# Three PSUM banks of the v blocks and one SyncE transfer are moved in a cross-attention and feed-forward kernel

## The reference

```python
# x [8, 256, 256], ctx [8, 77, 256], 16 heads of 64
x = x + xattn(layernorm(x), ctx)     # LN with gamma, beta inside; then
                                     # q = xn @ w_q; k, v = split(ctx @ w_kv)
                                     # softmax(q k^T / 8) v; @ w_out + b_out; * tanh(gate)
x = x + ffn(layernorm(x))            # (silu(x wg^T) * (x wu^T)) wd^T, 256 -> 768 -> 256,
                                     # int32 weights times 1/127
```

## Time and profile before

| what | value |
|---|---|
| median of 3 runs | 317.37 us (316.65 to 319.08) |
| profiled execution | 316.46 us, span of its instructions 314.6 us |
| TensorE matmul busy | 298.3 us, 95% |
| VectorE, ScalarE, GpSimd busy | 235.3, 172.2, 167.0 us |
| granted clock of TensorE | 0.999 |
| DMA | 23.29 MB, mean 74 GB/s |

### The profile page before, as it was taken

The page is one execution under the profiler, slowest core; times in us unless marked ns, Lnnn a source line. Parts: engine busy times, 40 slices in busy tenths (PEclk is TensorE's granted clock), DMA queues, the critical chain, the costliest instruction groups (busy, mean ns, idle before and its releaser), DMA issues.

```text
span 314.6 us, 6453 instructions
## 1 busy us (share of the span) xinstructions
PE 298.3 (95%) x2399; PEld 275.8 (88%) x2399; DVE 235.3 (75%) x622; ACT 172.2 (55%) x338; POOL 167.0 (53%) x170
## 2 busy tenths in 40 slices
PE   7799999897987999999999999999999999989896
PEld 7798977686885999889988989898999889978896
DVE  1298887596785887878887797778787878784873
ACT  4356874658325852773486249535942772465142
POOL 2390863347853871668096629644771668045042
PEclk9999999999999999999999999999999999999999
DMA  6993153512414021102201120202020101100001
GB/s 201 387 361 84 35 205 138 174 52 102 138 55 118 2 73 35 33 3 74 68 0 32 44 69 0 76 0 69 1 77 33 35 0 43 56 13 0 2 0 70
DMA packets 16314, 23.29 MB, mean 74 GB/s; under 512 B 1634, under 2 KB 13898, under 8 KB 16282
## 3 DMA queue, kind: packets, MB, share of 16 engines
q1 hardware_dynamic: 16282, 22.85, 22.3%
HBM read 15.87 MB, written 4.62 MB: 65 GB/s over the span
## 4 chain that ended last, share of the span: by engine, by line
PE 80%; POOL 10%; issue 3%; DVE 2%; ACT 2%; DMA 2%; SPq 0%; POOLq 0%; ACTq 0%; DVEq 0%
PE ps L825 11%; PE ps L771 8%; PE ps L757 7%; PE ps L731 5%; PE ps L739 5%; PE ps L735 5%; PE ps L658 4%; PE ps L886 4%; PE ps L890 4%; PE ps L887 4%; PE ps L844 3%; PE ps L873 3%; PE ps L870 3%; POOL probs L1127 3%; POOL t_lo L1134 3%
## 5 line engine op out<-in xcount | busy, mean ns | idle before, releaser
L1127 POOL TENSOR_TENSOR probs<-probs,total 128x616 f32<-128x616 f32 x32 | 39.1, 1221 | 75.7 <-DVE total L1260 75.7
L978 ACT COPY pt<-ps 77x512 f32<-77x512 f32 x64 | 34.2, 584 | 49.2 <-PE ps L757 49.2
L1134 POOL TENSOR_TENSOR t_lo<-t_all,t_hi 128x1232 fp32r<-128x1232 f32 x16 | 45.6, 2849 | 4.7 <-ACT t_hi L1003 4.7
L1143 POOL TENSOR_TENSOR h_lo<-hid,h_hi 128x256 fp32r<-128x256 f32 x42 | 31.0, 737 | 28.4 <-ACT h_hi L1053 28.4
L757 PE MATMUL ps<-ident,probs 128*77 128x128 f32 x256 | 33.3, 273 | 4.3 <-POOL probs L1127 3.0
L886 PE MATMUL ps<-wo_hi,o_hi 128*128 128x256 f32 x128 | 36.3, 284 | 0.0
L887 PE MATMUL ps<-wo_lo,o_hi 128*128 128x256 f32 x128 | 36.1, 282 | 0.0
L890 PE MATMUL ps<-wo_hi,o_lo 128*128 128x256 f32 x128 | 36.0, 281 | 0.0
L1243 DVE TENSOR_REDUCE top<-ps 128x4 f32<-128x308 f32 x64 | 28.7, 472 | 9.4 <-PE ps L739 9.2
L757 PEld LDWEIGHTS ps<-ident,probs 128*77 128x77 f32 x256 | 29.5, 147 | 5.4 <-POOL probs L1127 3.7
L731 PE MATMUL ps<-t_hi,xn_hi 128*128 128x308 f32 x128 | 30.7, 321 | 0.7 <-ACT v_out L937 0.7
(11 more groups left out here) (152 smaller groups left out, 819.3 us busy)
## 6 DMA issues: line engine op xcount, KB each, us to landing
v<-v_scratch SPq DMA_DIRECT2D x8, 308.0 KB
x_ln<-in_x SPq DMA_DIRECT2D x8, 256.0 KB, 4.5
v_scratch<-v_out SPq DMA_DIRECT2D x4, 512.0 KB, 2.9
stream<-in_x SPq DMA_DIRECT2D x8, 256.0 KB, 2.8
x_rooms<-in_x SPq DMA_DIRECT2D x7, 256.0 KB, 7.8
out<-stream SPq DMA_DIRECT2D x7, 256.0 KB, 2.2
wk_raw<-in_L_xattn_w_kv SPq DMA_DIRECT2D x4, 256.0 KB, 4.9
wq_raw<-in_L_xattn_w_q SPq DMA_DIRECT2D x1, 1024.0 KB, 7.7
```

The costliest lines, as they stand in the source:

```text
L978: nc.scalar.copy(pt[:, q * HB:(q + 1) * HB, t * P:(t + 1) * P], ps_p[0:K, m % 2, :].rearrange("k (h q) -> k h q", h=HB)).then_inc(pt_copie ...
L1127: nc.gpsimd.tensor_tensor(p, p, total[:, u, :].unsqueeze(2).to_broadcast([P, HG, K]), ALU.mult).then_inc(probs_done, 1)
L1134: nc.gpsimd.tensor_tensor(t_lo[:, :, cols], t_all[:, :, n, cols], t_hi[:, :, cols].bitcast(F32), ALU.subtract).then_inc(tlo_done, 1)
```

## The change

Three edits. (1) v7 goes to bank 4 instead of 6, v8 to bank 3 instead of 4, v9 to bank 6 instead of 5. The waits of S1 and of T0 are cut to the blocks that hold the banks they write: S1 waits for v3 (bank 2) and no more for v4 (bank 3); T0 waits for the last holders of banks 4 and 5, which are now v7 and v6, and no more for v9. So v7 waits for the copy of v5, v8 for that of v4, v9 for that of v2 (before: v2, v5, v6). (2) On SyncE the copy wd_t to wd moves behind the load of x_ln for batch 2. (3) As that load no longer stands behind the copy, ScalarE's and GpSimd's h0 of round 1 (which write where wd_t lies) wait for the copy's landing.

```diff
-SP_ORDER = "RES V LN OUT".split()
+SP_ORDER = "RES V LN WD OUT".split()
...
-V_BANKS = (4, 5, None, 2, 3, 4, 5, None, 4, 5)
+V_BANKS = (4, 5, None, 2, 3, 4, 5, 4, 3, None)
...
                 sp.dma_start(v[:], v_scratch.rearrange("(b k) n -> b k n", k=K)[n]).then_inc(v_in, 16)
-                if isinstance(n, int) and n == 1:
-                    weights_in_place(2)
...
-            stages = {"RES": ("now", load_res), "LN": ("next", lambda n: load_ln(n + 1)),
+            stages = {"RES": ("now", load_res), "LN": ("next", lambda n: load_ln(n + 1)), "WD": ("first", weights_in_place, 2),
...
                 if isinstance(b, int) and b == 0 and u == 1:
-                    for n in range(first_v, last_v + 1):
-                        if V_BANKS[n - first_v] in (2, 3):
-                            evacuated(pe, n)
+                    evacuated(pe, first_v + V_BANKS.index(SCORE_BANKS[2]))
...
                 if isinstance(b, int) and b == 0 and u == 0:
-                    for n in range(last_v - 2, last_v + 1):
-                        evacuated(pe, n)
+                    for at in (4, 5):
+                        evacuated(pe, last_v - V_BANKS[::-1].index(at))
...
             def split_h(b, f):
+                if b == 1 and f == 0:
+                    act.wait_ge(s_wf[2], 16)
...
             def split_h(b, f):
+                if b == 1 and f == 0:
+                    pool.wait_ge(s_wf[2], 16)
```

## The result

| | before | changed |
|---|---|---|
| median of 6 runs each, us | 317.24 (316.17 to 319.08) | 312.07 (311.85 to 312.32) |
| ratio | 1 | 0.984 (95% interval 0.982 to 0.987) |
| profiled execution, us (its span) | 316.46 (314.6) | 312.03 (310.2) |

The forecast was 312.8, range 311.3 to 315.0. Two things in the table want an explanation: the 4.4 us, and why the medians differ by 0.8 us more. The second is visible in the table already: the runs of before spread over 2.9 us, those of the changed kernel over 0.5 us.

The account below looks back on a forecast made before the run. TensorE, busy every microsecond from 106.7 to 280, bounds the kernel, so earlier gains arrive nearly whole. 1.9 + 2.3 = 4.2 us off gave 312.3 (profiled) and 313.2 (median); the forecast was their middle, 312.8, range 311.3 to 315.0.

Parts of the forecast that it names:

- What bounds the kernel: TensorE, busy every microsecond from 106.7 to 280 us, so a gain made before 106.7 should reach the end nearly whole.
- S1: On TensorE, S1 waits for v3 alone, so its 0.66 hole goes: 0.7 us, with v5 to v9 following 0.7 earlier.
- T0: On TensorE, an earlier register load and branch move T0 from 61.05 to about 59.15: 1.9 us, S1's 0.7 included.
- (a): Rival at T0: something other than v6's copy holds the load; T0 gains 0.7, total 3.0, as a middle 313.9; chance 0.14.
- The branch: TensorE's sequencer branch ahead of T0 still takes 3.7 us and is over at 58.7 to 59.0; growing longer would be wrong.
- C0 behind Ta: On ScalarE, C0 gains only 0.8, but T1's slack of 0.25 to 0.35 lets the 1.9 pass.
- SyncE's order: Earlier x_ln load removes TensorE's holes of 1.3, 0.6 and 0.2 in round 1: 2.3 us, lower bound 1.3.
- h0's wait: Round 1's h0 on ScalarE and GpSimd waits for wd: cost nothing, with 4.5 us of cover.
- The sum: Whole kernel: 1.9 + 2.3 = 4.2 us, giving 312.3 from the profiled execution, 313.2 from the median.
- (b): Rival in round 1: another late comer keeps x_lo's or P3's hole open; total gain 3.2, 313.7; chance 0.08.
- (c): Rival at round 1's end: something tied to DMA or another engine holds it, no gain, 316.5; chance 0.05.
- (d): Rival at h0: wd lands late and holds both engines, costing 4.0 of the 4.2, or slower, about 319; chance 0.03.

Follow-up runs that it names:

- e4: The changed kernel with T0's wait on v9's copy put back: 312.31 us (4 runs), span 310.4.
- e3: The changed kernel with a wait for v6's copy added on TensorE ahead of the register load: 312.56 us (4 runs), span 310.8.
- e5: The changed kernel with v7 in bank 3, v8 in bank 6, v9 in bank 7, none waiting for a copy later than v4's: 312.33 us (6 runs).
- e2: The kernel before with only the x_ln load moved ahead of wd and h0's waits, banks as before: 313.66 us (6 runs), ratio 0.990.
- e9: The kernel before, unchanged, profiled again: 315.71 us, clock 1.0.
- e10: The kernel before with x_ln of batch 2 loaded still later, behind wd and the residual of batch 1: 317.75 us (10 runs), ratio 1.004.
- e11: The kernel before, unchanged, profiled once more: 317.15 us, mean clock 0.994.
- e1: The kernel before with only the new banks of v7 to v9 and the cut waits of S1 and T0: 314.80 us (12 runs), ratio 0.994.
- e6: The changed kernel with SyncE's copy of the down weights held until round 1's first tanh: 316.36 us (one run), span 314.5.

## Why the prediction was right, point by point
**What bounds the kernel.** Right: nothing behind T3 of round 1 ate or added anything of weight (0.1 of the 4.4 is from there).

**S1.** Forecast 0.7, measured 0.93 (50.91 to 49.98), and v5 to v9 followed 0.9 earlier. The idle bracket of 0.66 counts from the modelled end of the transpose ahead; without the hole S1 starts 0.03 behind that transpose's start. So a hole here cost some 0.25 more than its bracket.

**T0.** The reading held at its central points: the branch, not v9's copy, ended last (e4), and what had held the branch was the register load behind v9's wait on v6's copy (e3 brings it back). The term was mis-sized by 0.25: 1.66 for 1.9. The load stood at 54.57 for 54.25 to 54.5, it and the branch took 0.07 and 0.10 longer than before, and T0 followed the branch by 0.17 for 0.25. I let the load follow v5's copy by 0.1 to 0.35, since six matmuls had passed in 0.07; it came 0.6 behind. e5 shows that v5's copy was not the holder: with that wait gone as well the load stands in the same place, with 17 matmuls ahead of it. Rival (a) had named a full queue as the holder, and I argued it down. As the holder of the kernel before it was wrong (there 14 were left when the load came, and it came with v6's copy), as the next holder in line it fits: e5 finds the sequencer 17 matmuls ahead of the array at two places. What sets this distance no run here shows. The Trainium skill (Advanced Engine Details and Errata, Engine Queue Depths) gives TensorE 64 entries; 17 matmuls with their weight loads are 34, so a queue full at 64 is not what the rows show.

**The branch.** Forecast as fixed at 3.67. It took 3.77 in the changed kernel; over the profiles it is 3.37 to 3.67 in before, e2, e9, e10, e11 and 3.57 to 3.91 in all those in which the load comes earlier. So coming earlier goes with some 0.3 more, which the forecast had as a danger and not in the sum; why it does is open. The profiled execution of before had the longest branch of its kind, 0.3 above the other four; measured against the end of v4's copy, T0 of the kernel before usually stands at 10.0 behind it (10.28 in that execution) and that of the changed kernel at 8.64. The typical gain of edit 1 at T0 is 1.35, about midway between rival (a)'s 0.7 and my 1.9; the other 0.3 of the 1.66 is chance in the pair of profiles. Against that, e1's runs at full clock give 1.8; no run here settles which is nearer.

**C0 behind Ta.** The slack forecast as 0.25 to 0.35 held: T1 follows T0 by 2.60, as before.

**SyncE's order.** Right in each step: issue at 81.02, no wait at LN, the holes of 1.3, 0.6 and 0.2 gone, X done and P3 in time. Forecast 2.3, measured 2.65 from T0 to T3: the three holes are 2.1 by their brackets, and the rest, 0.5, is again some 0.2 for each, where I had put 0.1. Seen from the other side: before, T0 to T3 is 45.61, changed 42.96. This part is the firm one: e9 has 45.63 again, and e2 to e5 have 42.94 to 42.98.

**h0's wait.** No cost, as forecast, with the cover of 4.5 that was reckoned; e6 shows the price without it: 0.5 of slack first, then T3 late, and the clock on top.

**The sum.** 4.2 forecast for the profiled execution, 4.43 measured: 0.25 too much at T0, 0.35 too little at the turn, and 0.1 behind T3, with S1's surplus inside T0's figure. That the sum came so near is in part luck: errors of opposite sign met, and the long branch in the profiled execution of before hid 0.3 of the miss at T0. For the medians I had added nothing, and they moved by 5.2. The other 0.8 is most likely the clock. Where the clocks of before's runs are on record, their median lies in a mixture of runs at full clock (316.50 in the largest set, 316.57 and 316.22 in the others, 4.2 to 4.5 above the changed kernel's 312.07, much as the profiles say) and runs with the fall (317.45 in the largest set). For the six runs of before in the result they are not on record, so this is inferred. The changed kernel's six were all at full clock. That was no term of my sum, though the holes that I removed were in it. Part of the 0.8 is chance in which runs were drawn: beside the later kernels before's median was 316.44 and 316.61.

**The rivals.** (a) would have given T0 0.7: it gave 1.66, typically 1.35. (b) wanted x_lo or P3 late: neither hole stayed. (c) and (d) didn't occur; (d)'s mechanism is real, but it starts at a landing 4.5 us later than it was, and its price is higher than I put it: 4.3 of span for 3.2 of delay in e6's one run.

## What to carry to other kernels
When the profile puts a wait to an engine's last write, look at the distance: 0.14 was a release here, 0.38 to 0.68 was something else, a branch of the sequencer that the list of waits doesn't show. A bank, or any buffer, chosen for a block early in a queue decides when the sequencer gets to what stands far behind it; choose so that the last blocks ahead of a branch wait for the oldest copies. Load ahead of a transfer that waits for late work, whatever needs no such wait, and price a short hole on TensorE at more than its length, for the clock may fall behind it.

## What the runs showed that I had not expected
- TensorE's granted clock can fall to 0.50 for 3.4 us at or behind holes of 1.25 and 0.60 us (e1, e11) or 1.95 and 0.61 (e10) or 2.38 (e6), in some executions of the same kernel and not in others; matmul pairs then go at 0.43 for 0.235. It cost 0.9 us in e1's profile, 1.0 in e11's, 1.6 in e6's.
- The sequencer's branch took 3.4 to 3.9 us, while the array worked on.
- With no wait on v6's copy ahead of it, the register load came when 17 matmuls were still to start, however early the waits ahead of it were satisfied, and so did the wait ahead of v9 in e5.
